# Mamba scan and linear attention on one core: B and C rows held once, ten state buffers, three of sixteen C products per batch on GpSimd

## The reference

```python
xn = layernorm(x) * (1 + scale) + shift          # scale, shift, gate = silu(c) @ ada_w
x_in, z = split(xn @ in_proj)                    # 512 + 512 channels
u = silu(causal_conv4(x_in) + conv_b)
dt_r, B, C = split(u @ x_proj)                   # 64, 16, 16
dt = softplus(dt_r @ dt_proj + b);  A = -exp(A_log)
h[t] = h[t-1] * exp(dt[t] * A) + (dt[t] * u[t]) * B[t]     # 512 x 16 states
y[t] = sum over n of h[t, :, n] * C[t, n]  + u * D
x1 = x + gate * ((y * silu(z)) @ out_proj)
```

## Time and profile before

| | us |
|---|---|
| median of 3 runs | 667.79 |
| lowest, highest | 666.66, 671.83 |
| the profiled execution | 668.15 |
| its span in the trace | 666.3 |

### The profile page before, as it was taken

How to read it: one execution, slowest core, us unless ns; L and a number is a source line. 1 busy time by engine, 2 the same in 40 slices (tenths; PEclk the granted TensorE clock), 3 DMA queues, 4 the chain that set the end, 5 groups by cost and what they waited for, 6 DMA issues and landing times.

```text
span 666.3 us, 7102 instructions
## 1 busy us (share of the span) xinstructions
PE 452.1 (68%) x2352; PEld 376.6 (57%) x2352; DVE 589.3 (88%) x618; ACT 405.9 (61%) x874; POOL 389.4 (58%) x292
## 2 busy tenths in 40 slices
PE   3848687678566756778567856776666956775764
PEld 3637566566465645666456745665665756654642
DVE  4809999999999999999999999999999999999321
ACT  2374756558655868387755866487737774754232
POOL 4066759547855786557845694657746696661100
PEclk9978876898689789889689778989789966877886
DMA  7273042002400070005200160007000240000000
GB/s 214 70 248 122 1 162 92 1 16 78 178 1 0 19 268 1 0 17 179 92 0 13 50 226 1 0 16 260 12 0 1 82 190 0 1 16 1 0 16 17
DMA packets 19870, 44.31 MB, mean 67 GB/s; under 512 B 2348, under 2 KB 11060, under 8 KB 19829
## 3 DMA queue, kind: packets, MB, share of 16 engines
q1 hardware_dynamic: 19832, 43.84, 18.9%
HBM read 41.48 MB, written 2.36 MB: 66 GB/s over the span
## 4 chain that ended last, share of the span: by engine, by line
DVE 58%; issue 14%; PE 11%; ACT 9%; POOL 6%; DMA 1%; DVEq 0%; SPq 0%; ACTq 0%; POOLq 0%
DVE ring L635 33%; DVE hs L639 8%; DVE conv L625 5%; POOL hs L383 4%; PE YT L940 3%; ACT ring L504 3%; PE PY L983 2%; DVE st L605 2%; DVE yt L646 2%; DVE kmax L682 2%; PE PX L901 1%; ACT L455 1%; PE PX L836 1%; PE PY L1024 1%; ACT L578 1%
## 5 line engine op out<-in xcount | busy, mean ns | idle before, releaser
L383 POOL TENSOR_TENSOR hs<-dtu,BC 128x1024 f32<-128x1024 f32 x128 | 299.7, 2358 | 107.8 <-PE YT L940 107.7
L635 DVE TENSOR_TENSOR_SCAN ring<-ring,hs 128x1024 f32<-128x1024 f32 x128 | 292.1, 2282 | 20.2 <-POOL hs L383 16.2
L504 ACT ACTIVATE ring<-dt,Aneg 128x256 f32<-128x256 f32 x512 | 213.2, 464 | 149.2 <-DVE hs L639 149.1
L940 PE MATMUL YT<-ident,hs 128*128 128x128 f32 x1024 | 160.0, 312 | 51.5 <-DVE hs L639 51.4
L940 PEld LDWEIGHTS YT<-ident,hs 128*128 128x128 f32 x1024 | 139.9, 163 | 67.6 <-DVE hs L639 62.5
L639 DVE TENSOR_TENSOR hs<-ring,BC 128x1024 f32<-128x1024 f32 x128 | 156.8, 1225 | 4.4
L901 PE MATMUL PX<-xnT,win 128*128 128x256 f32 x232 | 67.0, 439 | 27.2 <-ACT xnT L435 11.2
L901 PEld LDWEIGHTS PX<-xnT,win 128*128 128x128 f32 x232 | 48.8, 222 | 39.9 <-ACT xnT L435 13.6
L983 PE MATMUL PY<-wqkvo,xT 128*128 128x256 f32 x192 | 63.3, 489 | 0.0
L983 PEld LDWEIGHTS PY<-wqkvo,xT 128*128 128x128 f32 x192 | 49.5, 258 | 10.2
L362 POOL TENSOR_TENSOR dt<-dt,conv 128x512 f32<-128x512 f32 x16 | 20.3, 1271 | 53.0 <-ACT conv L484 53.0
(11 more groups left out here) (126 smaller groups left out, 601.4 us busy)
## 6 DMA issues: line engine op xcount, KB each, us to landing
BC<-bc_rows SPq DMA_DIRECT2D x32, 1024.0 KB, 10.1
xg<-in_x SPq DMA_DIRECT2D x8, 256.0 KB, 2.8
out<-fin SPq DMA_DIRECT2D x8, 256.0 KB, 12.3
BC<-in_ada_wT SPq DMA_DIRECT2D x3, 512.0 KB, 5.0
win<-in_in_wT SPq DMA_DIRECT2D x2, 512.0 KB, 6.7
BC<-in_W_emb SPq DMA_DIRECT2D x2, 512.0 KB
wo<-in_out_wT SPq DMA_DIRECT2D x1, 512.0 KB, 13.0
bc_rows<-xdbl SPq DMA_DIRECT2D x8, 32.0 KB, 1.5
```

The source lines that it names most:

```text
L383: nc.gpsimd.tensor_tensor(hs[:, g % DBUF], dtu[:, b % 2, dc, :].unsqueeze(1).to_broadcast([P, NQ, T]), BC[:, b % 2, NQ * q:NQ * q + NQ, :] ...
L504: ins = nc.scalar.activation(ring[:, g % 2, j, :], dt[:, b % 2, dc, :], ACT.Exp, scale=Aneg[:, c:c + 1])
L635: V.tensor_tensor_scan(states, states, driven, 0.0, ALU.mult, ALU.add).then_inc(s_scan_done, 1)
L940: ins = M(YT[:, c, :], hs[:, g % DBUF, j, P * c:P * c + P], ident[:, :], is_transpose=True, start=False, stop=(q == UPC - 1 and j == NQ - ...
```

## The change

1. **B and C once.** `BC` (two copies of 32 rows) becomes `Br` and `Cr` (one copy of 16 rows each). `broadcast_bc` issues eight DMAs of 512 KB: the four groups of B first, each once POOL has read the old rows for the last time, then the four of C, each once the last product with the old rows is done. The weights that were staged in `BC` at the start are staged in `hs`.
2. **Ten buffers** `hs` in place of five.
3. **Units 5, 9 and 13 of a batch are multiplied by C on POOL.** For them the scan writes into `hs` and DVE goes on; POOL does `states_times_c` five places later in its list (after `inputs_of` of unit g + 5); PE sums that unit after its successor. The ring slot is free when the scan is done.
4. **z lies by tokens.** `in_proj_2` and `_3` are two matmuls each with 512 columns in place of four with 256. DVE's `copy_sums` becomes `gate_y(b, dc)`, a product of YT with zs (256 elements) in the same place; the two products at i = 3 go, and ACT copies the two banks instead (`copy_yg`, at i = 3 of ACT's list).
5. **Attention.** `max_qk` lets the reduction turn the sign (L682 goes). The sums of q over a head are four more matmuls ahead of `k_times_v`, each with 4 columns; DVE's reduction L686 goes, and the reciprocal moves to `head_blocks`.
6. **Gate rows** are stored to memory and loaded, one batch at a time, by SP; `setup_gates` and `gate_rows` go. `setup_emb` moves from g = 0 to g = -2.
7. POOL's slots: `softplus_0` and `_1` at -1 and 1, `residual` 26, `rstd1` 28, `rstd2` 40.

```diff
-DBUF, XBUF = 5, 3
+DBUF, XBUF = 10, 3
+def by_pool(g):
+    return g % U in (5, 9, 13)
+def summed_after(g):
+    return g - 1 if g >= 1 and by_pool(g - 1) else None
+def sums_until(g):
+    return g + 2 if by_pool(g) else g if g >= 1 and by_pool(g - 1) else g + 1
 # SP
+            def broadcast_b(b, q):
+                if b >= 1:
+                    sp.wait_ge(s_dbu_ready, U * b - UPC + q + 1)
+                sp.dma_start(Br[:, NQ * q:NQ * q + NQ], ...).then_inc(b_loaded[q], 16)
+            def broadcast_c(b, q):
+                if b >= 1:
+                    last = U * b - UPC + q
+                    if by_pool(last):
+                        sp.wait_ge(s_hc_pool, pool_units(last + 1))
+                    else:
+                        sp.wait_ge(s_hc_dve, dve_units(last + 1))
+                sp.dma_start(Cr[:, NQ * q:NQ * q + NQ], ...).then_inc(c_loaded[q], 16)
 # POOL
                 if g >= DBUF:
-                    pool.wait_ge(s_y_acc, g - DBUF + 1)
+                    pool.wait_ge(s_y_acc, sums_until(g - DBUF))
+            def states_times_c(b, i):
+                g, q = U * b + i, i % UPC
+                pool.wait_ge(s_scan_done, g + 1)
+                if i < 2 * UPC:
+                    pool.wait_ge(c_loaded[q], 16 * (b + 1))
+                nc.gpsimd.tensor_tensor(hs[:, g % DBUF], hs[:, g % DBUF], Cr[:, NQ * q:NQ * q + NQ, :],
+                                        ALU.mult).then_inc(s_hc_pool, 1)
+                if 0 <= g - BEHIND < NB * U and by_pool(g - BEHIND):
+                    states_times_c((g - BEHIND) // U, (g - BEHIND) % U)
-                for slot, step in ((-17, rstd0), (-3, softplus_0), (-1, softplus_1), (24, residual), (26, rstd1),
-                                   (38, rstd2)):
+                for slot, step in ((-17, rstd0), (-1, softplus_0), (1, softplus_1), (26, residual), (28, rstd1),
+                                   (40, rstd2)):
 # ACT
                 if g >= 2:
-                    act.wait_ge(s_hc_ready, g - 1)
+                    if by_pool(g - 2):
+                        act.wait_ge(s_scan_done, g - 1)
+                    else:
+                        act.wait_ge(s_hc_dve, dve_units(g - 1))
+            def copy_yg(b):
+                for h, bank in ((0, PZ), (1, PY)):
+                    act.wait_ge(s_yback_mm, 2 * b + h + 1)
+                    if b >= 1:
+                        act.wait_ge(s_out_mm, b)
+                    nc.scalar.activation(yg[:, 2 * h:2 * h + 2, :], bank[:, :, :], ACT.Copy).then_inc(s_yg_ready, 1)
-                                   (25, normalize1), (26, norm1), (30, exp_qk), ...
+                                   (19, copy_yg), (25, normalize1), (26, norm1), (30, exp_qk), ...
 # DVE
+                V.tensor_tensor_scan(driven if by_pool(g) else decays, decays, driven, 0.0, ...)
+                if by_pool(g):
+                    return
-                V.tensor_copy(yt[:, dc], YT[:, :, :]).then_inc(s_yt_ready, 1)
-            def gate_y(b):
+                dve.wait_ge(s_z_ready, 3 * b + 3)
+                V.tensor_tensor(ygT[:, :, P * dc:P * dc + P], YT[:, :, :], zs[:, b % 2, :, P * dc:P * dc + P],
+                                ALU.mult).then_inc(s_ygT_ready, 1)
-                V.tensor_scalar(kmax[:, :], kmax[:, :], -1.0, None, ALU.mult).then_inc(s_kmax_ready, 1)
-            def sums_qk(b):
+            def sum_k(b):
                 dve.wait_ge(s_ke_ready, KD * (b + 1))
                 V.reciprocal(rk[:, :], ksum[:, :]).then_inc(s_krec_ready, 1)
 # PE
+                    for k in range(KD):
+                        ins = M(flat(xz_bank(b, h)), xnT[:, k, P * c:P * c + P], win[:, k, DI:2 * DI], ...)
+                for c in range(TC):
+                    for h in range(KD):
+                        M(PZ[:, 1, lo:lo + HEADS // KD], qT[:, h, P * c:P * c + P], blockmask[:, 0::DH], ...)
-                if 0 <= g < NB * U:
+                if 0 <= g < NB * U and not by_pool(g):
                     sum_states(g // U, g % U)
+                    if summed_after(g) is not None:
+                        sum_states(summed_after(g) // U, summed_after(g) % U)
```

More of the change, by code:

```diff
@@ L34 @@
 MASKED = 1e6
-DBUF, XBUF = 5, 3
+DBUF, XBUF = 10, 3
+BEHIND = 5
 THIRDS = (0, 64, 96)
@@ L59, in due, with pool_units, dve_units @@
     return b if at == 0 and 0 <= b < NB else None
+def by_pool(g):
+    return g % U in (5, 9, 13)
+def pool_units(g):
+    return sum(by_pool(i) for i in range(g))
+def dve_units(g):
+    return g - pool_units(g)
+def summed_after(g):
+    return g - 1 if g >= 1 and by_pool(g - 1) else None
+def sums_until(g):
+    return g + 2 if by_pool(g) else g if g >= 1 and by_pool(g - 1) else g + 1
 def build(nc, a, out):
@@ L92, in build @@
         gate8 = sb("gate8", [NB, D])
-        gate = sb("gate", [P, NB, D])
+        gate = sb("gate", [P, 2, D])
         mods = sb("mods", [P, 4 * KD, NB])
@@ L253, in xz_bank, with flat @@
             return (PX, PY, PZ, ring[:, 0, 0:2, :])[h] if b == 0 else PX
+        def flat(bank):
+            return bank.rearrange("p e t -> p (e t)")
         def over_batches(col):
@@ L322, in _ @@
                     load_x(b + 2)
+                if b + 1 < NB:
+                    load_gate(b + 1)
             sp.wait_ge(s_out_stored, 16 * NB)
@@ L780, in add_emb_bias @@
                     V.tensor_tensor(m1b[:, k, :], m1b[:, k, :], mods[:, 3 * KD + k, :], ALU.add).then_inc(s_emb_ready, 1)
-            def gate_rows(half):
-                dve.wait_ge(s_gate_mm, half + 1)
-                for i, bank in ((0, PY), (1, PZ)):
-                    b = NB // 2 * half + 2 * i
-                    V.tensor_copy(gate[:, b:b + 2, :], bank[:, :, :]).then_inc(s_gate_ready, 1)
-            def gate_rows_0():
-                gate_rows(0)
-            def gate_rows_1():
-                gate_rows(1)
             def conv_taps_0(b):
@@ L806, in _ @@
                     if b is not None:
-                        copy_sums(b, dc)
-                for slot, step in ((-23, stats0), (-16, conv_taps_0), (-14, conv_taps_1), (19, gate_y), (21, gate_x),
-                                   (22, stats1), (27, max_qk), (29, sums_qk), (32, head_blocks), (33, normalize_q),
+                        gate_y(b, dc)
+                for slot, step in ((-23, stats0), (-16, conv_taps_0), (-14, conv_taps_1), (21, gate_x),
+                                   (22, stats1), (27, max_qk), (29, sum_k), (32, head_blocks), (33, normalize_q),
                                    (34, stats2), (40, finish)):
@@ L815, in _ @@
                     setup()
-                for at, step in ((3, setup_gate8), (8, add_emb_bias), (11, gate_rows_0), (14, gate_rows_1)):
+                for at, step in ((3, setup_gate8), (8, add_emb_bias)):
                     if g == at:
@@ L1067, in _ @@
                         step(b)
-                for at, step in ((0, setup_emb), (8, setup_gates_0), (11, setup_gates_1)):
-                    if g == at:
-                        step()
+                if g == -2:
+                    setup_emb()
 def kernel(x, cond_2048, mask_BxSx1_fk1, L0_cond_ln_g, L0_cond_ln_b, L0_cond_ada_w, L0_cond_ada_b, L0_cond_in_proj_w,
```

161 lines of the change are left out of this document (82 added, 79 removed).

## The result

The changed kernel takes 642.61 us, the median of five runs (639.23 to 655.24). The kernel before, run beside it five times, took 669.43. The ratio is 0.960 with a 95% interval of 0.956 to 0.964: 4.0% faster, 26.8 us. The forecast was 635, with 622 to 645 for its own case and 615 to 652 as the range. So direction, mechanism and size hold; the time is 7.6 us over the forecast, and of the forecast gain of 33.4 us 6.6 are missing. Medians are of all executions, ratios only of those within 1.5% of the fastest of their kernel. The 655 us execution is used where it shows something that the other does not, and is called "the long execution".

The account below looks back on a forecast made before the run. DVE, busy 88% of the span, was taken to bound the kernel. Face value 56.1 us, less waits and plus small gains, left 33.4 off 668.15: 635 us, with 622 to 645 for its own case (0.59) and 615 to 652 overall.

Parts of the forecast that it names:

- Face value: DVE's list from first scan to last product: the work taken off, counted start to start, sums to 56.1 us.
- The sign turn: L682 on DVE, which waits for POOL's running instruction: removing the seven in the stretch gains 11.1 us.
- gate_x and unit 4: DVE waits 0.9 before unit 4's scan and 1.6 before gate_x; 12.3 us lost in batches 2 to 6.
- In batch 1 PE's clock is low: Batch 1, in_proj_2 taking 3.78: gate_x comes at 146.2 instead of 144.49, 4.2 us lost.
- Exponentials of k: At sum_k, i = 13, DVE waits 1.0 for ACT's exp_qk; 7.0 us lost over seven batches.
- Unit 8: DVE's wait of 0.56 for ACT at unit 8 goes, since silus start earlier: 2.8 us back.
- POOL: POOL's products by C reach PE in time, up to five units ahead: 0 lost, 24 us at most.
- SP's reload of C: C's group 1, loaded after unit 13's product on POOL and needed by product 17: hidden, 5 us to spare.
- the rival that it makes the kernel slower: C's group 1 lands late; from another 4.8 us per batch the kernel is slower, at 7 us 684; chance 0.05.
- The work does not leave DVE: Rival: each POOL product shuts DVE out for its length, 57 us in all, giving 692 us; chance 0.03.
- Start: First scan near 44.5, first product waiting for C until 48.3; 1.2 us of gain remain after PE's setup_emb.
- q sums and tail: Four matmuls ahead of k_times_v delay DVE's head_blocks: 1.2 us lost in batch 7, 2.0 in the tail.

Follow-up runs that it names:

- e2: The changed kernel with ACT's copy_yg one place later, at i = 4 of its list instead of 3: 634.96 us, ratio 0.947.
- e3: The changed kernel with ACT's copy_z one place earlier, at i = 4 of its list instead of 5: 634.94 us, ratio 0.948.
- e7: The changed kernel with units 9 and 13 alone on POOL, unit 5 multiplied by DVE again: 651.66 us, ratio 0.967.
- e1: The changed kernel again, nothing edited, for a second profile: median 641.12 us, ratio 0.957; its profiled execution took 639.81 us.
- e11: e10 with DVE's sum_k one place later, at i = 14: 619.48 us, ratio 0.925.
- e4: The changed kernel with both ACT copies, copy_z and then copy_yg, at i = 4 of its list: 630.61 us, ratio 0.942.
- e6: The changed kernel with only DVE's sum_k one place later, at i = 14 instead of 13: 646.39 us, ratio 0.969.
- e10: e4 with silu_h first instead of last in ACT's group silus: 626.85 us, ratio 0.938.
- e12: e10 with units 9 and 13 alone on POOL, unit 5 multiplied by DVE again: 633.1 us, ratio 0.947.
- e9: The changed kernel with eight unread transposes on PE at each of three places per batch: 647.95 us, ratio 0.970.

## Why the prediction was right, and where not

**Face value.** 56.1 forecast, 54.9 measured in DVE's busy time between the first scan and the last product, at the places named. The sign turn: right in sum, uneven by batch.

**gate_x and unit 4.** The argument, that ACT's copies delay decays(4) and that out_proj then comes late, holds to 0.1 us in the batches that are like the one it was worked out on the earlier trace rows, and its parts are borne out: e2 removes the wait before unit 4, e3 the one before `gate_x`, and e7 shows unit 5's product lost in that one. The term was undersized all the same, because of the step "In batch 1 PE's clock is low": I let the low level count in batch 1 only, since only there the kernel before shows a long in_proj_2. In that kernel the chain had slack: the long in_proj_2 of batch 1 left 1.33 us of wait before `gate_y` and none before `gate_x`, and out_proj ran at 3.62 in all of batches 1 to 6. The change spent the slack, and from then on a low stretch that meets the chain costs up to 3 or 4 us a batch (3.2 in batches 3 to 6 of the long execution). In e1 that is some 2.3 of the 5.1 us by which its span misses the forecast (0.7 in batch 1, 1.6 in batch 2); POOL in batch 1 (2.5) and the start (1.2) are more. Between e1 and the long execution it is the whole difference. What decides where the low stretches fall is open.

**Exponentials of k.** 1.0 forecast, 1.07 measured in batches 1 to 6 and 0.67 in batch 7; e11 gives them back.

**Unit 8.** The wait of 0.56 went, as forecast; in e4 it is back, once what came before it is faster.

**POOL.** "States_times_c(13) ends near 8 us after the product of unit 12, and PE asks for it at about 9" was right for batches 1 to 7. I worked it out on one batch and took it for all. At the end of batch 0, where DVE has no `max_qk` and no `rk` and so reaches the next batch 3.1 us sooner (see e1), the margin is negative by 1.87, and batch 1 pays 2.5.

**SP's reload of C, and the rival that it makes the kernel slower.** Gone: products wait for C only at the start, 0.2 at most (e3, e4, e6, e10 and e12), and never later.

**The work does not leave DVE.** Gone: 1225 and 2281 ns as before. The Trainium skill (Perfetto Trace Analysis, Optimizing Scalar/DVE Operations) warns that moving work between these two engines might not help, since they share a read port. Here POOL's running instruction held up the 128 by 2 sign turn, which took up to 1.99 us, but not the scans and products with one operand in SBUF, and moving the products did help.

**Start.** The first scan came at 43.9 to 48.0, forecast near 44.5. It waited for ACT's ring and not for POOL, and the wait for C until 48.3 that I had put behind it did not come. Of gain I expected 1.2 at unit 3; measured was between 2.0 lost (e11) and 2.1 gained (e3), and nothing in e1 (e9, with more on PE, is left out). The two conv steps waited 2.1 to 2.3 and up to 3.4 for ACT.

**q sums and tail.** 2.0 forecast, 1.6 measured in the tail; 1.2 forecast for batch 7, and 1.7 more waited there in e1 than before, 0.2 more in the long execution.

## What to carry to other kernels

An instruction taken off the bounding engine is worth its length minus what its next releaser is late: units 5, 9 and 13 of the same list were worth 0, 1.25 and about 0.2 us. Work the next late thing out place by place, in every kind of batch and not in one only, and ask of each chain that loses its slack what it does when the matrix engine runs at its low level. Moving four steps within their engines' lists was worth nearly as much here (23 us, from 642 to 619) as taking work away was (27 us).

## What the runs showed of the hardware

- PE's granted clock fell to 0.50 (1.2 GHz) for a few us at a time in every profiled execution, at places that differ between batches and between executions of one kernel; the mean over the span does not tell which execution is long (0.857 at 653.5 us, 0.859 at 638.0). Sixteen matmuls of 256 columns took 3.62 at the high level, and up to 6.71 where it had fallen. The waits ahead of the chain were alike (1.24 and 1.25), and eight more matmuls at three places did not hold the level.
- A GpSimd product of 128 by 1024 f32 with both operands full takes 2363 ns, the same as with one operand spread.
- A scan of 128 by 1024 takes 2280 ns into SBUF and 2281 into PSUM.
- A negating reduction took DVE 682 ns, as without the negation, and unlike the small multiplication by -1 it never waited for POOL's products.
